# A layer of a graph network: one constant for the limits of the node buffer, four parts instead of five, lap operations at another place

## Chip, cores and metric

The kernel runs on one core of a Trainium2 chip. The metric is the device time of one execution in microseconds (us), lower is better.

## What is computed

The reference is one layer with three branches: a graph convolution over 106,250 edges between 6,250 nodes, a linear attention over the nodes, and a layer of two experts chosen by a router. Cut to what matters here, the graph branch is:

```python
m = src_feats[src_idx] @ weights[:d] + edge_feats @ weights[d:]
deg = jax.ops.segment_sum(jnp.ones((m.shape[0],)), dst_idx, num_segments=num_dst)
norm = jnp.where(deg > 0, jax.lax.rsqrt(jnp.maximum(deg, 1.0)), 0.0)
h = jax.ops.segment_sum(m * norm[dst_idx][:, None], dst_idx, num_segments=num_dst)
...
xn = _layernorm(x, axis=-1)
x = x + gnn(xn, edge_attr_256, src, dst, ...) + mix(xn[None], ...)[0]
x = x + ffn(_layernorm(x, axis=-1)[None], ...)[0]
```

`src_feats` is `xn` (6,250 x 256, float32), and the edges are sorted by their destination `dst`. Self loops are among them, so every node has at least one edge.

## The kernel before

**Edges and strips.** The sorted edges are cut into 277 strips (`NS`) of 384 edges (128 partitions x `TS` = 3), and four strips make a step, so there are 70 steps (`NG`), each of three loads of one edge per partition and strip. For a strip, POOL gathers the source rows from HBM by index (L554), SP loads the edge rows beside them (L418), and PE multiplies both by a one-hot matrix of 32 columns, one for each node from the strip's first (L887). This needs all destinations of a strip to lie within 32 nodes (`W`). The rows go through `ring`, which has six slots (`RS`). PE turns the strip's sums (L898), and DVE adds them into the node buffer `acc` at the row of the strip's first node (L1279); that row is read from `brow` into a register.

**The node buffer.** `acc` holds the sums of 5 x 250 nodes (`RC` x `CN` = `RN` = 1,250), and 32 more columns for strips that reach over its end. Node n stands at n modulo 1,250. The nodes are 25 parts of 250. When the last strip of a part has been added (`DONE`), DVE takes the degrees, ACT the root, DVE scales the part, PE projects it (`project`), ACT stores the result and clears the columns (`refill`). Before the strips of a step are added, DVE waits until the parts that are due have been cleared (`EMPTIED`, by the step alone). Where a part starts at column 0 again, `spill` (L1285, L1287) adds the 32 spare columns to the first 32 and clears them.

**The check.** The fast path is right only if each strip starts neither before the first part that is still open nor too far beyond it. `bwide` holds the first node of each strip. POOL writes two rows of 277 numbers, the lower limits `floor` (L547) and the upper limits `roof` (L550), by memsets of a few columns each; DVE subtracts, takes the maximum of both differences and reduces it to one flag, `ok_i`, which every engine reads at the end of the edge loop: with 0, a slow general path would run. `laps` counts how many times 1,250 goes into the first node, by one comparison for each lap (L1201, L1206); L1210 takes that off, and L1217 writes `brow`. `s_rel` is raised after `brow` and stands for all of it.

**The opening.** SP loads x in five blocks of ten tiles. DVE computes the statistics of each block (`stats`, L1133 to L1138), ACT takes the root, DVE the reciprocals (`scales`), and ACT normalises eight tiles and DVE two (`block_rest`, L1150). SP writes each block to the table `xn_table` in HBM. The order on DVE is written by hand: blocks 0, 1, 2, then the checks and laps, then blocks 3 and 4. Meanwhile POOL gathers the first 24 strips' rows from raw x into the ring. DVE takes their statistics in two halves (`raw_stats`), ACT the root of each half (L646), DVE the reciprocals (`raw_scales`, L1168), and ACT normalises twelve tiles of the ring for each half (L650). So DVE's second `raw_scales` waits until ACT has done the first half's twelve tiles. Then come `one_hot` (L1240) for step 0, the preparation of the weights, which SP loads behind the first six edge loads, the sum of two bias rows (L1267), and `one_hot` for step 1 in the loop.

Of the kernel before, what the change touches and what calls it, by code (L numbers as in the profile page):

```python
# [5 lines left out]
ALU = mybir.AluOpType  # L6
# [9 lines left out]
N = 6250  # L16
# [5 lines left out]
CN = 2 * TN  # L22
# [17 lines left out]
RC = 5  # L40
# [30 lines left out]
assert len(set(DONE)) == NC  # L71
# [9 lines left out]
def gps_layer(nc, x, src_l, dst_l, edges, wgnn, hbias, wkv_l, wq_t, bkv_l, bq_l, kln_g, kln_b, vln_g, vln_b,  # L81
              w1, b1_l, w2, b2, wr, br, fw1, fb1_l, fw2, fb2, gamma, beta, out):
    ctx = ExitStack()
    with ctx:
# [147 lines left out]
        roof = fl_t[:, :, :].rearrange("p c n -> p (c n)")[0:1, 0:NS]  # L232
# [10 lines left out]
        def wide(ap, n, m):  # L243
# [12 lines left out]
        s_id, s_const, s_iota, s_mask, s_d, s_dp, s_rel, s_wprep, s_roof, s_lap = (sem(f"s_{n}") for n in (  # L256
            "id", "const", "iota", "mask", "d", "dp", "rel", "wprep", "roof", "lap"))
# [270 lines left out]
        def _(pool):  # L528
# [19 lines left out]
            for e in sorted(set(EMPTIED)):  # L548
                lo, hi = EMPTIED.index(e) * ST, min((NG - EMPTIED[::-1].index(e)) * ST, NS)
                pool.memset(roof[0:1, lo:hi], float(CN * (e + RC) - W)).then_inc(s_roof, 1)  # L550

# [574 lines left out]
        def _(v):  # L1126
# [72 lines left out]
            v.wait_ge(s_roof, len(set(EMPTIED)))  # L1199
            v.tensor_tensor(roof[0:1, :], bwide[0:1, :], roof[0:1, :], ALU.subtract).then_inc(s_d, 1)  # L1200
            v.tensor_scalar(laps[0:1, 0, :], bwide[0:1, :], float(RN), None, ALU.is_ge).then_inc(s_lap, 1)  # L1201
            v.wait_ge(s_d, 11)
            v.tensor_tensor(floor[0:1, :], floor[0:1, :], roof[0:1, :], ALU.max).then_inc(s_d, 1)
            for k in range(2, N // RN + 1):
                v.wait_ge(s_lap, k - 1)
                v.scalar_tensor_tensor(laps[0:1, (k + 1) % 2, :], bwide[0:1, :], float(k * RN), laps[0:1, k % 2, :], ALU.is_ge, ALU.add).then_inc(s_lap, 1)  # L1206
            v.wait_ge(s_d, 12)
            v.tensor_reduce(okc[0:1, 5:6], floor[0:1, :], AX, ALU.max).then_inc(s_d, 1)
            v.wait_ge(s_lap, N // RN)
            v.scalar_tensor_tensor(laps[0:1, N // RN % 2, :], laps[0:1, (N // RN + 1) % 2, :], -float(RN), bwide[0:1, :], ALU.mult, ALU.add).then_inc(s_lap, 1)  # L1210
            v.wait_ge(s_d, 13)
            v.scalar_tensor_tensor(okc[0:1, 6:7], okc[0:1, 5:6], 0.0, okc[0:1, 4:5], ALU.is_le, ALU.mult).then_inc(s_d, 1)
# [427 lines left out]
```

## Time and profile before

| | us |
|---|---|
| median of three timed runs | 1610.42 |
| lowest and highest | 1605.93, 1611.3 |
| the profiled execution | 1606.38 |
| its span, first to last instruction | 1604.5 |

The page of the profile shows one execution. Its first part gives the busy time of each engine, its fourth the chain of work that ended last, followed back from the end. The windows give the busy time in chosen stretches, with the clock granted to PE as a share of full speed and the mean busy share of the DMA engines. An instruction's row has its start, its busy time, its line and operation, and in brackets how long its engine was idle before it and what ended that. "issue" and "remote" are idle times for which the profile names no instruction or transfer.

### The profile page before, as it was taken

The numbers are of one execution on the slowest core, as the hardware profiler recorded it, in microseconds if no ns is written. First come the engines' busy times: TensorE is split into PE (matmuls) and PEld (weight loads), VectorE is DVE, ScalarE is ACT, GpSimd is POOL, SyncE is SP. The second block draws the span as 40 slices with busy tenths as digits, with TensorE's granted clock in tenths as the row PEclk, the third lists the DMA queues.
The fourth block names the chain that finished last, engine by engine and source line by source line (L and its number), as shares of the span: only waits on it lengthen the run. The fifth ranks groups of instructions, "written<-read, shape, count | busy, mean of one in ns | idle before, by whom it ended". The sixth has DMA issues, their size and how long they took to land.

```text
span 1604.5 us, 19853 instructions
## 1 busy us (share of the span) xinstructions
PE 1070.4 (67%) x5959; PEld 659.1 (41%) x5959; DVE 757.2 (47%) x1750; ACT 539.1 (34%) x1100; POOL 933.1 (58%) x999
## 2 busy tenths in 40 slices
PE   0154775765677575666656675665666649999997
PEld 0011332322223222233333342333334349999997
DVE  5643453444544454423334343343343446677675
ACT  5511111211111111112233342343333356767673
POOL 6066766766776676666666667666676003434342
PEclk9977876868798787778867789787887869999999
DMA  9775655565665565487777778777776131111111
GB/s 270 261 227 164 199 182 180 173 191 174 193 185 182 172 195 171 142 248 208 219 217 229 216 246 249 210 232 227 222 249 202 46 93 28 50 46 44 50 39 40
DMA packets 189375, 275.65 MB, mean 172 GB/s; under 512 B 19840, under 2 KB 160296, under 8 KB 188037
## 3 DMA queue, kind: packets, MB, share of 16 engines
q1 hardware_dynamic: 139424, 152.85, 31.8%
q0 software_dynamic: 39888, 108.97, 22.6%
q10 hardware_dynamic: 9975, 12.80, 2.4%
q8 instruction: 37, 0.61, 0.2%
q14 instruction: 51, 0.42, 0.1%
HBM read 248.95 MB, written 25.60 MB: 171 GB/s over the span
## 4 chain that ended last, share of the span: by engine, by line
PE 37%; another core or an unknown queue 25%; issue 16%; DVE 12%; ACT 5%; DVEq 2%; DMA 1%; SPq 0%; ACTq 0%; POOL 0%; POOLq 0%
PE bank L1097 8%; PE bank L887 6%; PE bank L1086 5%; PE ps_t L1086 4%; PE bank L998 3%; PE bank L955 3%; PE bank L986 3%; PE bank L910 2%; DVEq L1277 2%; DVE acc L1279 2%; DVE lnst L1314 1%; DVE xc L1310 1%; PE ps_t L898 1%; PE bank L977 1%
## 5 line engine op out<-in xcount | busy, mean ns | idle before, releaser
L554 POOL DMA_INDIRECT ring<-xn_table,src_sb x807 | 798.2, 989 | 405.6 <-issue 225.4
L887 PE MATMUL bank<-ring,s 128*32 128x512 f32 x1662 | 285.8, 670 | 94.6 <-DVE s L1240 48.8
L955 PE MATMUL bank<-wstage,xt 128*125 128x512 f32 x200 | 135.6, 814 | 121.0 <-ACT xt L620 104.4
L1279 DVE TENSOR_TENSOR acc<-acc,ps_t 128x160 f32 x277 | 89.2, 322 | 141.2 <-issue 88.1
L887 PEld LDWEIGHTS bank<-ring,s 128*32 128x32 f32 x1662 | 42.8, 115 | 223.5 <-issue 166.5
L910 PE MATMUL bank<-wg,acc 128*125 128x256 f32 x400 | 102.2, 412 | 33.8 <-DVE acc L1302 29.8
L689 ACT ACTIVATE kvn<-xc 125x512 f32<-125x512 f32 x50 | 31.5, 630 | 263.6 <-DVE xc L1310 173.1
L1531 DVE TENSOR_TENSOR h_lo<-h,h_hi 128x512 fp32r<-128x512 f32 x100 | 95.7, 968 | 49.1 <-ACT h_hi L620 49.1
L1249 DVE TENSOR_TENSOR pair<-s 128x128 f32<-128x128 f32 x70 | 20.4, 292 | 208.5 <-remote 158.9
L609 POOL TENSOR_TENSOR rx<-vex,half 125x2 f32<-125x2 f32 x25 | 17.5, 701 | 171.9 <-DVE nmx L1552 171.9
L955 PEld LDWEIGHTS bank<-wstage,xt 128*125 128x125 f32 x200 | 44.1, 245 | 169.5 <-ACT xt L620 113.8
L1097 PE MATMUL bank<-fw_hi,h_hi 128*125 128x256 f32 x400 | 111.7, 279 | 0.0
L1097 PE MATMUL bank<-fw_hi,h_lo 128*125 128x256 f32 x400 | 111.7, 279 | 0.0
L1097 PE MATMUL bank<-fw_lo,h_hi 128*125 128x256 f32 x400 | 111.6, 279 | 0.0
L910 PEld LDWEIGHTS bank<-wg,acc 128*125 128x125 f32 x400 | 79.5, 204 | 73.3 <-DVE acc L1302 39.0
L998 PE MATMUL bank<-w_sb,hm 128*125 128x256 f32 x200 | 66.0, 487 | 59.7 <-ACT hm L704 37.9
L620 ACT ACTIVATE xt<-bank 128x250 f32<-128x250 f32 (+1 forms) x75 | 33.4, 445 | 198.1 <-remote 163.6
L1310 DVE TENSOR_TENSOR xc<-bank,bkv 125x512 f32<-125x512 f32 x50 | 34.4, 689 | 122.9 <-remote 108.5
L620 ACT ACTIVATE fl<-bank 128x512 f32<-128x512 f32 x70 | 41.2, 589 | 139.1 <-remote 102.0
L986 PE MATMUL bank<-xt,p_sb 128*128 128x250 f32 x200 | 61.8, 463 | 38.8 <-issue 37.2
L998 PEld LDWEIGHTS bank<-w_sb,hm 128*125 128x125 f32 x200 | 45.5, 239 | 92.2 <-ACT hm L704 45.9
L1097 PEld LDWEIGHTS bank<-fw_hi,h_hi 128*125 128x125 f32 x400 | 74.3, 186 | 0.0
(211 smaller groups left out, 2216.5 us busy)
## 6 DMA issues: line engine op xcount, KB each, us to landing
ring<-edges SPq DMA_DIRECT2D x207, 512.0 KB
ring<-xn_table,src_sb POOLq DMA_INDIRECT x807
xnr<-xn_table SPq DMA_DIRECT2D x25, 250.0 KB
xch<-x SPq DMA_DIRECT2D x25, 250.0 KB
base_rows<-xch ACTq DMA_DIRECT2D x25, 250.0 KB
xt_cols<-xte ACTq DMA_DIRECT2D x25, 250.0 KB
xtl<-xt_cols SPq DMA_DIRECT2D x25, 250.0 KB, 5.0
out<-res SPq DMA_DIRECT2D x25, 250.0 KB
```

The source lines that it names most:

```text
L554: pool.indirect_dma_start(out=to, out_offset=None, in_=rows, in_offset=bass.IndirectOffsetOnAxis(ap=index, axis=0),).then_inc(done, 16)
L620: return nc.scalar.activation(o, i, ACT.Copy)
L887: mm = pe.matmul(ps_seg[t % 2][j * W:(j + 1) * W, :], lhsT=s32[:, t % 3, j * TS + i, :], rhs=ring[:, u, j, :], start=i == 0, stop=i == TS ...
L910: mm = pe.matmul(ps_f[0:TN, j * D:(j + 1) * D], lhsT=acc[:, o, a:a + TN], rhs=wg[:, o, :], start=o == 0, stop=o == 2 * KC - 1)
L955: mm = pe.matmul(ps_kv[0:TN, :], lhsT=xt[:, n % 2, c, 0:TN], rhs=wstage[:, c, :], start=c == 0, stop=c == KC - 1)
L986: mm = pe.matmul(ps_kv[:, f * CW:f * CW + CN], lhsT=p_sb[:, o, f * P:(f + 1) * P], rhs=xt[:, (NT + c) % 2, o, :], start=o == 0, stop=o == ...
L998: mm = pe.matmul(ps_acc[0:TN, j * D:(j + 1) * D], lhsT=hm[:, f, j * TN:(j + 1) * TN], rhs=w2_sb[:, f, :], start=f == 0, stop=f == KC - 1)
L1086: mm = pe.matmul(bank[q][:, (f % 2) * CW:(f % 2 + 1) * CW], lhsT=a, rhs=b, start=n == 0, stop=n == len(ops) - 1)
L1097: mm = pe.matmul(ps_o[u][0:TN, j * D:(j + 1) * D], lhsT=a, rhs=b, start=n == 0, stop=n == len(ops) - 1)
L1279: v.tensor_tensor(acc[:, :, ds(b, W)], acc[:, :, ds(b, W)], planes[:, :, j * W:(j + 1) * W], ALU.add).then_inc(s_acc, 1)
L1310: v.tensor_tensor(xc[:, :], ps_kv[0:TN, :], bkv[:, :], ALU.add).then_inc(s_xc, 1)
L1531: v.tensor_tensor(h_lo[:, u, 2 * q:2 * q + 2, :], h32[:, 2 * q:2 * q + 2, :], h_hi[:, u, 2 * q:2 * q + 2, :].bitcast(F32), ALU.subtract).t ...
```

## The change

The buffer has four parts of 250 nodes instead of five (`RC`). The upper limits are gone, and POOL's 25 memsets with them: DVE subtracts the first nodes from `floor` and reduces the difference twice, to its maximum (which must not be above 0) and to its negated minimum (which must not be above 3 x 250 - 32 = 718). An assertion at build time says that the parts due to be cleared at a step are at most one behind the parts that are done. The flag now raises `s_rel`. The lap operations, one more of them because 1,000 goes into 6,250 six times, and the cast to `brow` stand between the two `raw_scales`, and raise a semaphore `s_ok` for which DVE waits before the first add.

```diff
-RC = 5
+RC = 4
...
-assert len(set(DONE)) == NC
+assert len(set(DONE)) == NC and all(EMPTIED[g] >= sum(d <= g for d in DONE[:-1]) - 1 for g in range(NG))
...
-            for e in sorted(set(EMPTIED)):
-                lo, hi = EMPTIED.index(e) * ST, min((NG - EMPTIED[::-1].index(e)) * ST, NS)
-                pool.memset(roof[0:1, lo:hi], float(CN * (e + RC) - W)).then_inc(s_roof, 1)
...
             v.tensor_tensor(floor[0:1, :], floor[0:1, :], bwide[0:1, :], ALU.subtract).then_inc(s_d, 1)
-            v.wait_ge(s_roof, len(set(EMPTIED)))
-            v.tensor_tensor(roof[0:1, :], bwide[0:1, :], roof[0:1, :], ALU.subtract).then_inc(s_d, 1)
-            v.tensor_scalar(laps[0:1, 0, :], bwide[0:1, :], float(RN), None, ALU.is_ge).then_inc(s_lap, 1)
-            v.wait_ge(s_d, 11)
-            v.tensor_tensor(floor[0:1, :], floor[0:1, :], roof[0:1, :], ALU.max).then_inc(s_d, 1)
-            for k in range(2, N // RN + 1):
-                v.wait_ge(s_lap, k - 1)
-                v.scalar_tensor_tensor(laps[0:1, (k + 1) % 2, :], bwide[0:1, :], float(k * RN), laps[0:1, k % 2, :], ALU.is_ge, ALU.add).then_inc(s_lap, 1)
+            v.wait_ge(s_d, 10)
+            v.tensor_reduce(okc[0:1, 5:6], floor[0:1, :], AX, ALU.max).then_inc(s_d, 1)
+            v.tensor_reduce(okc[0:1, 6:7], floor[0:1, :], AX, ALU.min, negate=True).then_inc(s_d, 1)
             v.wait_ge(s_d, 12)
-            v.tensor_reduce(okc[0:1, 5:6], floor[0:1, :], AX, ALU.max).then_inc(s_d, 1)
...
+            v.scalar_tensor_tensor(okc[0:1, 7:8], okc[0:1, 5:6], 0.0, okc[0:1, 4:5], ALU.is_le, ALU.mult).then_inc(s_d, 1)
             v.wait_ge(s_d, 13)
-            v.scalar_tensor_tensor(okc[0:1, 6:7], okc[0:1, 5:6], 0.0, okc[0:1, 4:5], ALU.is_le, ALU.mult).then_inc(s_d, 1)
+            v.scalar_tensor_tensor(okc[0:1, 5:6], okc[0:1, 6:7], float(CN * (RC - 1) - W), okc[0:1, 7:8], ALU.is_le, ALU.mult).then_inc(s_d, 1)
             v.wait_ge(s_d, 14)
-            v.tensor_copy(ok_i[:, :], okc[0:1, 6:7]).then_inc(s_d, 1)
...
-            v.tensor_copy(brow[0:1, :], laps[0:1, N // RN % 2, :]).then_inc(s_rel, 1)
+            v.tensor_copy(ok_i[:, :], okc[0:1, 5:6]).then_inc(s_rel, 1)
...
             raw_scales(0)
+            v.tensor_scalar(laps[0:1, 0, :], bwide[0:1, :], float(RN), None, ALU.is_ge).then_inc(s_lap, 1)
+            for k in range(2, N // RN + 1):
+                v.wait_ge(s_lap, k - 1)
+                v.scalar_tensor_tensor(laps[0:1, (k + 1) % 2, :], bwide[0:1, :], float(k * RN), laps[0:1, k % 2, :], ALU.is_ge, ALU.add).then_inc(s_lap, 1)
...
+            v.tensor_copy(brow[0:1, :], laps[0:1, N // RN % 2, :]).then_inc(s_ok, 1)
             raw_scales(1)
```

The order on DVE in the opening, from the subtraction of the first nodes to the statistics of block 3. Before (`fl` is `floor`, `fl_t` is `roof`, `kvn` holds `laps`):

```order
L1198 TENSOR_TENSOR fl<-fl,bwide 1x277
L1200 TENSOR_TENSOR fl_t<-bwide,fl_t 1x277
L1201 TENSOR_SCALAR kvn<-bwide 1x277
L1203 TENSOR_TENSOR fl<-fl,fl_t 1x277
L1206 SCALAR_TENSOR_TENSOR kvn<-bwide,kvn 1x277 x4
L1208 TENSOR_REDUCE okc<-fl 1x1
L1210 SCALAR_TENSOR_TENSOR kvn<-kvn,bwide 1x277
L1212 SCALAR_TENSOR_TENSOR okc<-okc 1x1
L1214 CAST ok_i<-okc 1x1
L1217 CAST brow<-kvn 1x277
L1219 CAST iota<-iota_i 128x128
L1133 BN_STATS st<-x 125x6 x10
```

Now:

```order
L1194 TENSOR_TENSOR fl<-fl,bwide 1x277
L1196 TENSOR_REDUCE okc<-fl 1x1
L1197 TENSOR_REDUCE okc<-fl 1x1
L1199 SCALAR_TENSOR_TENSOR okc<-okc 1x1
L1201 SCALAR_TENSOR_TENSOR okc<-okc 1x1
L1203 CAST ok_i<-okc 1x1
L1205 CAST iota<-iota_i 128x128
L1129 BN_STATS st<-x 125x6 x10
```

Nine operations left this place, and a second reduction and a second one-element combination came in.

Later on DVE, from the first `raw_scales` to the second and on to `one_hot` of step 0. Before:

```order
L1168 RECIPROCAL rg<-sdg 128x12
L1170 SCALAR_TENSOR_TENSOR nmrg<-mvg,rg 128x12
L1168 RECIPROCAL rg<-sdg 128x12
L1170 SCALAR_TENSOR_TENSOR nmrg<-mvg,rg 128x12
L1240 TENSOR_TENSOR s<-iota,rel 128x384
```

Now:

```order
L1164 RECIPROCAL rg<-sdg 128x12
L1166 SCALAR_TENSOR_TENSOR nmrg<-mvg,rg 128x12
L1216 TENSOR_SCALAR kvn<-bwide 1x277
L1219 SCALAR_TENSOR_TENSOR kvn<-bwide,kvn 1x277 x5
L1221 SCALAR_TENSOR_TENSOR kvn<-kvn,bwide 1x277
L1223 CAST brow<-kvn 1x277
L1164 RECIPROCAL rg<-sdg 128x12
L1166 SCALAR_TENSOR_TENSOR nmrg<-mvg,rg 128x12
L1234 TENSOR_TENSOR s<-iota,rel 128x384
```

The eight lap operations stand between the two.

In the edge loop the spills are at parts 4, 8, 12, 16, 20 and 24 instead of 5, 10, 15 and 20. On DVE at part 4, between the last add of a step and the degrees (`nrm`), the order now is:

```order
L1274 TENSOR_TENSOR acc<-acc,ps_t 128x5x32
L1280 TENSOR_TENSOR acc<-acc 128x5x32
L1282 MEMSET acc 128x5x32
L1289 TENSOR_SCALAR nrm<-acc 128x250
L1234 TENSOR_TENSOR s<-iota,rel 128x384
```

Two operations have come in there. On the other engines only POOL's 25 memsets of `fl_t` are gone, and ACT's first clearing of `acc` has 5,160 instead of 6,410 elements in a row. PE and SP have the same instructions in the same order.

## Rows read from the trace of the kernel before

**Rows 1.** The page, parts 1 and 4: busy time of the engines; the chain by engine

```profile
PE 1070.4 (67%) x5959; PEld 659.1 (41%) x5959; DVE 757.2 (47%) x1750; ACT 539.1 (34%) x1100; POOL 933.1 (58%) x999
...
PE 37%; another core or an unknown queue 25%; issue 16%; DVE 12%; ACT 5%; DVEq 2%; DMA 1%; SPq 0%; ACTq 0%; POOL 0%; POOLq 0%
```

**Rows 2.** Windows: length, busy time and instructions by engine, granted clock, DMA share, GB/s

```profile
60.00:80.00 20.00, 4.58 (x26) 1.12 (x26) 9.79 (x52) 12.77 (x28) 1.88 (x2) 1.00 0.98 309
400.00:1200.00 800.00, 523.33 (x2403) 258.18 (x2403) 329.50 (x772) 206.65 (x409) 546.28 (x554) 0.81 0.70 210
1300.00:1604.00 304.00, 286.26 (x2404) 285.48 (x2404) 200.69 (x360) 204.83 (x426) 106.60 (x100) 0.97 0.17 48
```

**Rows 3.** The chain of waits: start us, length us, what

```profile
67.99 6.00 ACT ring L650 x12
```

**Rows 4.** DVE's instructions: start, busy, operation, idle time before and its releaser

```profile
15.55 1.02 DVE L1179 TENSOR_TENSOR rel<-rel,bwide 128x831 f32<-128x831 f32 x1
...
35.01 0.43 DVE L1198 TENSOR_TENSOR fl<-fl,bwide 1x277 f32<-1x277 f32 x1
...
38.42 0.43 DVE L1203 TENSOR_TENSOR fl<-fl,fl_t 1x277 f32<-1x277 f32 x1 [2.41 <-remote]
39.83 0.43 DVE L1206 SCALAR_TENSOR_TENSOR kvn<-bwide,kvn 1x277 f32<-1x277 f32 x1 [0.97 <-remote]
42.62 0.44 DVE L1206 SCALAR_TENSOR_TENSOR kvn<-bwide,kvn 1x277 f32<-1x277 f32 x1 [2.36 <-issue]
44.02 0.43 DVE L1206 SCALAR_TENSOR_TENSOR kvn<-bwide,kvn 1x277 f32<-1x277 f32 x1 [0.96 <-issue]
44.71 0.44 DVE L1206 SCALAR_TENSOR_TENSOR kvn<-bwide,kvn 1x277 f32<-1x277 f32 x1 [0.26 <-issue]
45.08 0.42 DVE L1208 TENSOR_REDUCE okc<-fl 1x1 f32<-1x277 f32 x1
45.43 0.43 DVE L1210 SCALAR_TENSOR_TENSOR kvn<-kvn,bwide 1x277 f32<-1x277 f32 x1
...
46.67 3.33 DVE L1133 BATCH_NORM_STATS2 st<-x 125x6 f32<-125x256 f32 x10
```

**Rows 5.** Windows of the opening

```profile
40.00:45.00 5.00, 0.00 (x0) 0.00 (x0) 1.42 (x4) 0.00 (x0) 1.90 (x3) 1.00 0.93 363
45.00:50.00 5.00, 0.00 (x0) 0.00 (x0) 4.75 (x18) 0.00 (x0) 0.00 (x0) 1.00 0.20 75
50.00:55.00 5.00, 0.00 (x0) 0.00 (x0) 4.93 (x26) 3.82 (x9) 0.00 (x0) 1.00 0.55 178
55.00:60.00 5.00, 0.00 (x0) 0.00 (x0) 4.89 (x26) 4.12 (x10) 0.00 (x0) 1.00 0.74 240
```

**Rows 6.** Around the weights: waits, and instructions of DVE, PE and SP's queue

```profile
DVE st L1133 <- DMA x<-x: 4.7, 1, 4.7
...
50.79 0.73 DVE L1150 TENSOR_SCALAR x<-x,r,nmr 125x256 f32<-125x256 f32 x2
...
88.44 0.44 DVE L1267 TENSOR_TENSOR brows<-brows,hrows 125x256 f32<-125x256 f32 x1 [3.65 <-DMA hrows<-hbias]
...
89.58 1.94 PE L887 MATMUL bank<-ring,s 128*32 128x512 f32 x8 [9.93 <-issue]
...
62.03 8.01 SPq L418 DMA_DIRECT2D ring<-edges  x6
70.09 1.21 SPq L437 DMA_DIRECT2D wstage<-wkv_l  x1
```

**Rows 7.** DVE's wait for the second root

```profile
74.12 0.23 DVE L1168 RECIPROCAL rg<-sdg 128x12 f32<-128x12 f32 x1 [6.17 <-ACT sdg L646]
```

**Rows 8.** POOL's first gather

```profile
12.37 1.16 POOL L554 DMA_INDIRECT ring<-x,src_sb  x1 [6.26 <-issue]
```

**Rows 9.** DVE at the first spill, L1285 and L1287

```profile
401.21 0.33 DVE L1285 TENSOR_TENSOR acc<-acc 128x160 f32<-128x160 f32 x1
...
401.86 0.29 DVE L1294 TENSOR_SCALAR nrm<-acc 128x250 f32<-128x250 f32 x1
```

More of the change, by code:

```diff
@@ L231, in gps_layer @@
         floor = fl[0:1, 0:NS]
-        roof = fl_t[:, :, :].rearrange("p c n -> p (c n)")[0:1, 0:NS]
         laps = kvn[:, :, :].rearrange("p a d -> p (a d)")[0:1, 0:2 * NS].rearrange("p (a s) -> p a s", a=2)
@@ L255, in gps_layer @@
         s_gst, s_gmv, s_gve, s_gsd, s_grc, s_gr, s_raw = (sem(f"s_{n}") for n in ("gst", "gmv", "gve", "gsd", "grc", "gr", "raw"))
-        s_id, s_const, s_iota, s_mask, s_d, s_dp, s_rel, s_wprep, s_roof, s_lap = (sem(f"s_{n}") for n in (
-            "id", "const", "iota", "mask", "d", "dp", "rel", "wprep", "roof", "lap"))
+        s_id, s_const, s_iota, s_mask, s_d, s_dp, s_rel, s_wprep, s_ok, s_lap = (sem(f"s_{n}") for n in (
+            "id", "const", "iota", "mask", "d", "dp", "rel", "wprep", "ok", "lap"))
         s_e, s_gat = ([sem(f"s_{n}{u}") for u in range(RS)] for n in ("e", "gat"))
@@ L1229, in _ @@
             raw_scales(0)
+            v.tensor_scalar(laps[0:1, 0, :], bwide[0:1, :], float(RN), None, ALU.is_ge).then_inc(s_lap, 1)
+            for k in range(2, N // RN + 1):
+                v.wait_ge(s_lap, k - 1)
+                v.scalar_tensor_tensor(laps[0:1, (k + 1) % 2, :], bwide[0:1, :], float(k * RN), laps[0:1, k % 2, :], ALU.is_ge, ALU.add).then_inc(s_lap, 1)
+            v.wait_ge(s_lap, N // RN)
+            v.scalar_tensor_tensor(laps[0:1, N // RN % 2, :], laps[0:1, (N // RN + 1) % 2, :], -float(RN), bwide[0:1, :], ALU.mult, ALU.add).then_inc(s_lap, 1)
+            v.wait_ge(s_lap, N // RN + 1)
+            v.tensor_copy(brow[0:1, :], laps[0:1, N // RN % 2, :]).then_inc(s_ok, 1)
             raw_scales(1)
@@ L1269, in _ @@
             v.wait_ge(s_br, 1)
+            v.wait_ge(s_ok, 1)
             v.wait_ge(s_zero, 1)
```

4 lines of the change are left out of this document (removed).

## Prediction

> **What bounds the kernel now.** I read the page first, then the chain of waits in order of time, then the instructions of each engine in order of time around the changed lines. The page says that no engine is full over the whole span: PE is busy for 67% and POOL for 58% [rows 1]. The windows show three stages: an opening with hardly any matmul work up to 75 us, the edge loop up to about 1250 us with the DMA engines 70% busy over most of it, and an expert stage in which PE runs 286 of 304 us [rows 2]. The change touches the first, and two instructions more in the second; the third stays as it is.
>
> In the opening the chain of waits lies on DVE from the first block of x on: statistics, the checks, statistics again, then ACT's first twelve scalings of the ring at 67.99 us [rows 3]. In that chain the checks and lap operations, lines 1198 to 1219, take the stretch from 35.01 us to the next statistics at 46.67 us, 11.66 us [rows 4]. Little of it is work: five waits in brackets before these operations, 2.41, 0.97, 2.36, 0.96 and 0.26 us, make 6.96 us. Each of these operations waits for a semaphore that DVE's own previous operation raises; elsewhere such a wait is invisible (45.08 to 45.43 us). All the stalls that I see there end before 44.7 us, while the DMA engines are still 0.93 busy; from 45 us they are 0.20 busy and the stalls are gone [rows 4, 5].
>
> **What the checks lose.** Out of the stretch go the subtraction for the upper limit (L1200), the first comparison (L1201), the maximum (L1203), four lap comparisons (L1206), the lap product (L1210) and the cast to the row numbers (L1217). A second reduction and a second one-element operation come in. Without a stall, a 277-element operation costs 0.35 us from start to start (45.08 to 45.43) [rows 4]; I let the one-element ones cost no more. The new stretch is the subtraction, two reductions, two combinations and the flag's cast, 6 x 0.35 = 2.1 us, and the cast of iota, which stays as it is. That is 11.66 - 2.1 = 9.6 us less if no stall is left, and 9.6 - 7.0 = 2.6 us less if all of them return on other operations. These are the bounds of the main term.
>
> Between them: ten operations of the old stretch wait for DVE's own results and lose 6.96 us, 0.7 each; five of them lose 1.4 each. The new stretch has four such waits (first reduction, both combinations, the flag's cast), which makes 2.8 to 5.6 us of stall, and a gain of 4.0 to 6.8 us. Another way is to lay the new operations over the old stalls where they stood in time: the reductions run until 36.15 us, the first combination waits until 38.42, the second until 39.83, and the statistics begin at 40.4 us, 6.3 us early. I take 6.0 us.
>
> **Whether 6 us of DVE arrive at the end of the opening.** Block 3 of x must have landed at 40.4 us instead of 46.67; DVE waits for a block of x only once, before the first [rows 6], which says that block 3 is there by 46.67, not since when. The write of block 2 of the table follows DVE's last tiles of that block at 51.5 us [rows 6] and would come at 45.5 us. Between 45 and 60 us the DMA engines have 5 x (0.80 + 0.45 + 0.26) = 7.6 us free [rows 5], so that 6 us fit, but 9.6 would not quite: the gathers that now end by 47 us would share the engines with it. Behind it SP issues the edge loads from 62.03 and the weights from 70.09 us; the last row that DVE needs lands at 88.44 us, and behind it stands one_hot(1), for which PE's fourth group of strips waits until 89.58 us [rows 6]. From 60 to 80 us the DMA engines are 0.98 busy [rows 2], thus this part shifts with its start and doesn't shrink. A cap of about 7 us follows for any DVE gain, 6.0 passes.
>
> **The moved lap operations** stand between the two halves of the ring's scales, where DVE waits from 67.95 to 74.12 us, 6.17 us, for ACT's root [rows 7]. The first comparison, five instead of four further ones (1,000 goes into 6,250 six times), the product and the cast are 8 x 0.35 = 2.8 us. They cost nothing as long as they stay under 6.17 us. If stalls like those of the opening came back here, 2.8 + 7.0 = 9.8 us would pass the cover by 3.6 us, which would then delay ACT's second twelve tiles and one_hot(0). For it: the DMA engines are 0.98 busy there too [rows 2]. Against it: no operation of DVE that follows in the next twenty microseconds is late by its own predecessor; the ones that wait name a DMA or ACT [rows 6, 7].
>
> **POOL and ACT** lose the 25 memsets of L550 and a fifth of the clearing of acc. POOL's first gather starts 6.26 us after its last memset [rows 8], so the gathers may start sooner by the memsets' time or not at all; DVE reads what they bring only after all five blocks, ACT has nothing to do before DVE's first variance. I count zero for both.
>
> **The smaller buffer.** It spills at every fourth part of 250 nodes, thus six times instead of four. One spill pushes DVE's next operation from 401.21 to 401.86 us: 0.65 us [rows 9]. Two more are 1.3 us at most, and zero where DVE is waiting anyway. I take 0.6. The waits of the adds for emptied parts are by EMPTIED, which is the same table as before, so the smaller buffer brings no new wait.
>
> **The addresses.** All tiles behind acc move down by 5,024 bytes (20,640 instead of 25,640 bytes for acc, rounded up), so the ring starts 224 instead of 128 bytes above a multiple of 256. No row here shows a transfer to another start. The Trainium skill, DMA: Bandwidth & Descriptors, section How a descriptor splits into AXI transactions, speaks against this: a descriptor that starts off a 256-byte boundary is fetched from the boundary below, so that, if it held for writes into the ring as well, a row of 1,024 bytes would cost 39 beats of 32 bytes and not 36. I take zero and keep the case as a rival.
>
> **Sum.** -6.0 + 0.6 = -5.4 us. The profiled execution took 1606.38 us (span 1604.5), so 1601.0 for such a one. The three timed runs lie at 1605.93 to 1611.3 around a median of 1610.42; the profiled one is 4.0 below that, which by the median would give 1605.0. Between the two I say 1603.5.
>
> **Rivals.**
> 1. *The stalls return* on whatever waits in that window: gain 2.6 - 0.6 = 2.0 us, about 1607. For it: they lie in one stretch of time, the last before the DMA engines empty [rows 4, 5]. Against: there are fewer waits left to suffer.
> 2. *The stalls belonged to the removed operations*: they stand before operations with a scalar or a second operand from SBUF, none before the reduction or the statistics [rows 4]. Then up to 9.6 us go, of which the DMA engines pass about 7 to 9: 1600. The Trainium skill, SBUF — State Buffer, section Who interferes with whom, has such a rule: a DVE operation with two SBUF inputs or in a two-port mode is locked out while GpSimd holds the pair, a reduction never. The trace agrees only in part, since POOL generates gathers from 12.37 us on [rows 8], and the subtraction at 15.55 us, with two operands from SBUF, shows no stall [rows 4].
> 3. *The edge loop swallows it*: the loop waits on landings and on PE's granted clock (0.81 there, between its two levels of 1.2 and 2.4 GHz) [rows 2], so 6 us sooner in need not be 6 us sooner out: 1608 to 1610.
> 4. *Slower, by the addresses*: 25% of the chain is waits for an unknown queue, which in the loop are the gathers' and edges' landings [rows 1]. Transfers 5% longer would make 0.05 x 0.25 x 1604 = 20 us, 1622; from 1.4% on (5.4 us) it eats the gain.
> 5. *The new check refuses the data* and the general path runs: milliseconds. By the reference's own draw the first node of a strip is at most 394 above its lower limit, where 718 are allowed, and never below it; the flag stays 1.
>
> **Chances.** Forecast, 4 to 7 us carried through: 0.45. Rival 2: 0.15. Rival 1: 0.13. Rival 3: 0.17. Rival 4: 0.09, of which half under 1611. Rival 5 and others: 0.01. All run to run within some 2.5 us. A measurement of this kernel tells about 0.3%, 4.8 us, from no change: faster means under 1605.6. That holds for rival 2, two thirds of the forecast and a little of the others: 0.5. Slower, over 1615.3: 0.08. Same: 0.42. The range that leaves out two in ten goes from rival 2 with its scatter to rival 3: 1598 to 1611.
>
> **What would show it.** Right: statistics of block 3 start near 40.4 us (36.9 at the least, 44 at the most); ACT's ring tiles near 62 and 68.6 us with the lap operations inside DVE's wait; one_hot(1) near 82.5 us; PE's expert stage begins 5 us sooner and lasts as long. Wrong: the stalls on the new reductions, lap operations past the root, one_hot(1) at 88 us in spite of an earlier start (the DMA cap), or an edge loop that is longer by what the opening saves; for rival 4, a loop longer by 10 us or more with gathers' waits grown all over it.

## The result, and the profile after

| | before | after |
|---|---|---|
| median of 19 timed runs, us | 1607.81 | 1603.32 |
| lowest and highest | 1602.61, 1613.23 | 1597.46, 1610.02 |
| the profiled execution | 1606.38 | 1610.02 |
| its span | 1604.5 | 1608.2 |

The ratio after to before is 0.9972, with a 95% interval of 0.996 to 0.9983: 4.5 us less. The nineteen executions of after spread over 12.6 us, and the profiled one is the longest of them, so its length says nothing about the change; what can be read from it is where things stand in it. The page's parts 1 and 4, the answer to [rows 1]:

```profile
PE 1053.9 (66%) x5959; PEld 653.6 (41%) x5959; DVE 757.3 (47%) x1755; ACT 537.5 (33%) x1100; POOL 929.4 (58%) x974
...
another core or an unknown queue 31%; PE 30%; issue 14%; DVE 11%; ACT 8%; DMA 2%; DVEq 2%; SPq 2%; ACTq 0%; POOL 0%; POOLq 0%
```

The windows of after, for [rows 2] and [rows 5] (length, busy time and instructions of PE, PEld, DVE, ACT, POOL, granted clock, DMA share, GB/s):

```profile
60.00:80.00 20.00, 5.66 (x26) 1.20 (x26) 8.61 (x34) 12.99 (x27) 5.64 (x6) 0.97 1.01 302
400.00:1200.00 800.00, 504.63 (x2401) 250.79 (x2399) 324.67 (x764) 204.52 (x405) 548.11 (x554) 0.80 0.70 211
...
40.00:45.00 5.00, 0.00 (x0) 0.00 (x0) 4.90 (x23) 2.73 (x6) 0.00 (x0) 1.00 1.01 266
45.00:50.00 5.00, 0.00 (x0) 0.00 (x0) 4.93 (x25) 4.20 (x9) 0.00 (x0) 1.00 1.02 418
```

In the middle of the loop, instructions, clock (0.80 against 0.81) and DMA share are as before; PE shows 19 us less busy time there, which I leave unexplained. In the opening, DVE is busy for 4.90 of the 5 us from 40 us on, where before it had 1.42, and the quiet of the DMA engines behind 45 us (0.20) is gone.

DVE's instructions around the checks, for [rows 4] (start, busy, operation, in brackets the idle time before it and its releaser):

```profile
29.08 3.36 DVE L1129 BATCH_NORM_STATS2 st<-x 125x6 f32<-125x256 f32 x10
...
33.63 0.31 DVE L1132 BATCH_NORM_AGGREGATE mvs<-st 125x2 f32<-125x6 f32 x3 [1.04 <-DVE st L1129]
...
35.76 0.18 DVE L1132 BATCH_NORM_AGGREGATE mvs<-st 125x2 f32<-125x6 f32 x1 [1.21 <-remote]
...
38.00 0.17 DVE L1134 TENSOR_SCALAR ve<-mvs 125x10 f32<-125x10 f32 x1 [1.23 <-DVE mvs L1132]
...
39.44 0.43 DVE L1194 TENSOR_TENSOR fl<-fl,bwide 1x277 f32<-1x277 f32 x1
39.90 0.43 DVE L1196 TENSOR_REDUCE okc<-fl 1x1 f32<-1x277 f32 x1
40.26 0.42 DVE L1197 TENSOR_REDUCE okc<-fl 1x1 f32<-1x277 f32 x1
...
41.28 3.35 DVE L1129 BATCH_NORM_STATS2 st<-x 125x6 f32<-125x256 f32 x10
```

The stretch from the subtraction to the next statistics takes 41.28 - 39.44 = 1.84 us, where it took 11.66, and no wait is left in it. But it begins 4.4 us later than before (39.44 against 35.01). The stalls now stand before it, on the aggregation of block 2, an operation that has no scalar, yet they are not the reason: before the change 4.6 us of stall stood between the statistics of block 2 and the stretch as well (the 1.75, 1.81 and 1.06 us below), and now there are 4.4. The reason is that the statistics of block 2 begin 4.15 us later, at 29.08 us instead of 24.93. Before:

```profile
24.93 3.36 DVE L1133 BATCH_NORM_STATS2 st<-x 125x6 f32<-125x256 f32 x10
...
30.71 0.17 DVE L1138 TENSOR_SCALAR ve<-mvs 125x10 f32<-125x10 f32 x1 [1.75 <-remote]
...
33.52 0.17 DVE L1144 SCALAR_TENSOR_TENSOR nmr<-mvs,r 125x10 f32<-125x10 f32 x1 [1.81 <-remote]
...
34.94 0.14 DVE L1197 TENSOR_SCALAR okc<-okc 1x1 f32<-1x1 f32 x1 [1.06 <-issue]
```

Out of 9.8 us less in the stretch come 5.4 us at its end (41.28 against 46.67). Over the whole opening up to 50 us, DVE's stalls of 0.2 us or more, without its waits for loads, add up to 11.8 us before and 4.4 us after.

DVE in its wait for the second root, for [rows 7], and the step to `one_hot` of step 1, for [rows 6]:

```profile
62.89 0.29 DVE L1216 TENSOR_SCALAR kvn<-bwide 1x277 f32<-1x277 f32 x1
63.22 2.32 DVE L1219 SCALAR_TENSOR_TENSOR kvn<-bwide,kvn 1x277 f32<-1x277 f32 x5
65.57 0.44 DVE L1221 SCALAR_TENSOR_TENSOR kvn<-kvn,bwide 1x277 f32<-1x277 f32 x1
66.04 0.30 DVE L1223 CAST brow<-kvn 1x277 int32<-1x277 f32 x1
69.15 0.23 DVE L1164 RECIPROCAL rg<-sdg 128x12 f32<-128x12 f32 x1 [2.82 <-ACT sdg L642]
69.50 0.55 DVE L1234 TENSOR_TENSOR s<-iota,rel 128x384 f32<-128x384 f32 x1
...
88.23 0.42 DVE L1261 TENSOR_TENSOR brows<-brows,hrows 125x256 f32<-125x256 f32 x1 [5.31 <-issue]
88.75 0.56 DVE L1234 TENSOR_TENSOR s<-iota,rel 128x384 f32<-128x384 f32 x1
```

The eight lap operations take 62.89 to 66.34 us and leave 2.82 us of the wait: they are hidden. The sum of the bias rows comes no earlier than before (88.23 against 88.44). The chain of waits of after no longer passes ACT's ring tiles as in [rows 3]; it goes over SP's queue to the last row that this sum needs (start, length, what), although `one_hot` of step 0 is 5 us earlier (69.50 against 74.47):

```profile
58.05 2.16 SPq L417
...
77.16 0.62 SPq L445
...
77.83 7.85 DMA hrows<-hbias
```

POOL's last memset and its first gather, for [rows 8]; DVE at the first spill, for [rows 9]:

```profile
3.67 1.05 POOL L546 MEMSET fl<- 1x16 f32 x25
4.91 1.16 POOL L550 DMA_INDIRECT ring<-x,src_sb  x1 [0.18 <-issue]
```

```profile
343.48 0.33 DVE L1280 TENSOR_TENSOR acc<-acc 128x160 f32<-128x160 f32 x1
...
344.13 0.29 DVE L1289 TENSOR_SCALAR nrm<-acc 128x250 f32<-128x250 f32 x1
```

The first gather starts 7.5 us earlier than before, by far more than the 1.43 us that the removed memsets were busy. I had not expected that, and most of the study turns on it.

### The profile page after: what moved, and what is told of

It reads as the page before. It is cut to its first block, busy times and chain, and to the rows that moved or that the text cites. A ratio compares the mean times of both kernels' runs of the same rounds, so it can differ in the third digit from the quotient of the medians.

```text
span 1608.2 us, 19835 instructions
## 1 busy us (share of the span) xinstructions
PE 1053.9 (66%) x5959; PEld 653.6 (41%) x5959; DVE 757.3 (47%) x1755; ACT 537.5 (33%) x1100; POOL 929.4 (58%) x974
## 4 chain that ended last, share of the span: by engine, by line
another core or an unknown queue 31%; PE 30%; issue 14%; DVE 11%; ACT 8%; DMA 2%; DVEq 2%; SPq 2%; ACTq 0%; POOL 0%; POOLq 0%
PE bank L1093 8%; PE bank L1082 5%; PE ps_t L1082 4%; PE bank L883 3%; PE bank L951 3%; PE bank L906 2%; DVEq L1272 2%; PE bank L982 1%; DVE acc L1274 1%; DVE lnst L1309 1%; DVE nrm L1295 1%; DVE xc L1305 1%; PE bank L994 1%; DMA x<-x 1%
## 5 line engine op out<-in xcount | busy, mean ns | idle before, releaser
L550 POOL DMA_INDIRECT ring<-xn_table,src_sb x807 | 795.7, 986 | 416.4 <-issue 223.4
L883 PE MATMUL bank<-ring,s 128*32 128x512 f32 x1662 | 279.1, 678 | 82.8 <-DVE s L1234 53.3
L605 POOL TENSOR_TENSOR rx<-vex,half 125x2 f32<-125x2 f32 x25 | 17.5, 701 | 171.9 <-DVE nmx L1547 171.9
L616 ACT ACTIVATE xt<-bank 128x250 f32<-128x250 f32 (+1 forms) x75 | 33.5, 446 | 236.7 <-remote 198.3
L994 PE MATMUL bank<-w_sb,hm 128*125 128x256 f32 x200 | 62.0, 460 | 55.5 <-ACT hm L700 31.6
L594 POOL TENSOR_TENSOR xlb<-xl,b2w 125x512 f32<-125x512 f32 x25 | 32.4, 1297 | 73.2 <-DVE b2w L1589 73.2
```

The source lines that it names most:

```text
L550: pool.indirect_dma_start(out=to, out_offset=None, in_=rows, in_offset=bass.IndirectOffsetOnAxis(ap=index, axis=0),).then_inc(done, 16)
L616: return nc.scalar.activation(o, i, ACT.Copy)
L883: mm = pe.matmul(ps_seg[t % 2][j * W:(j + 1) * W, :], lhsT=s32[:, t % 3, j * TS + i, :], rhs=ring[:, u, j, :], start=i == 0, stop=i == TS ...
L994: mm = pe.matmul(ps_acc[0:TN, j * D:(j + 1) * D], lhsT=hm[:, f, j * TN:(j + 1) * TN], rhs=w2_sb[:, f, :], start=f == 0, stop=f == KC - 1)
```

## The experiments

I call "gate" the first gather from the table (L550 with `xn_table`), with which the edge loop's stream of gathers starts: 77.81 us before, 72.84 after. PE's first group of strips releases it:

```profile
72.84 0.95 POOL L550 DMA_INDIRECT ring<-xn_table,src_sb  x1 [37.60 <-PE bank L883]
```

In the table below, all times are us from the start of the span of one profiled execution each; the ratios are against the kernel before on the same chip, that of after from the result above and those of e1 to e10 from five timed rounds. e11 and e12 are profiles only. "Raw gathers" are the start of the first and the last of the 24 gathers from raw x; "last stall" is the last operation of DVE before 50 us that begins 0.2 us or more late after DVE's own previous one; "hot 1" is the start of `one_hot` for step 1; "25th" the 25th gather from the table.

| kernel | raw gathers | last stall | statistics of block 4 | gate | hot 1 | 25th | ratio, 95% interval |
|---|---|---|---|---|---|---|---|
| before | 12.37, 41.56 | 46.14 | 51.77 | 77.81 | 88.97 | 112.50 | 1 |
| before, again (e11) | 12.65, 42.29 | 44.24 | 49.70 | 75.75 | 86.62 | 108.90 | |
| after | 4.91, 34.29 | 38.00 | 46.39 | 72.84 | 88.75 | 108.33 | 0.9972, 0.996 to 0.9983 |
| e1 buffer of five parts | 4.91, 34.66 | 38.64 | 47.70 | 73.74 | 85.87 | 107.25 | 0.9978, 0.9965 to 0.999 |
| e3 old addresses | 4.91, 34.86 | 38.19 | 46.80 | 72.84 | 84.68 | 106.34 | 0.9977, 0.9964 to 0.999 |
| e6 bias rows later | 4.92, 34.16 | 38.55 | 47.21 | 73.25 | 81.13 | 107.35 | 0.998, 0.9965 to 0.9994 |
| e8 and weights sooner | 4.92, 34.44 | 38.49 | 46.86 | 72.91 | 76.77 | 106.50 | 0.9977, 0.9963 to 0.9991 |
| e2 memsets back | 12.08, 41.61 | 46.04 | 47.51 | 73.56 | 86.48 | 107.16 | 0.9998, 0.9982 to 1.0013 |
| the same again (e12) | 13.11, 42.20 | 45.34 | 50.65 | 76.69 | 89.51 | 110.10 | |
| e5 gathers held | 11.73, 41.60 | 46.04 | 47.09 | 73.13 | 86.48 | 107.23 | 1.0, 0.9984 to 1.0016 |
| e4 laps in front | 4.91, 34.51 | 38.95 | 50.69 | 76.73 | 89.05 | 110.24 | 1.0002, 0.9987 to 1.0016 |
| e7 memsets and laps in front | 13.21, 42.18 | 46.88 | 55.16 | 81.20 | 93.27 | 115.21 | 1.0012, 0.9998 to 1.0026 |
| e9 `one_hot(0)` sooner | 4.91, 34.79 | 38.63 | 47.01 | 69.80 | 87.33 | 106.88 | 0.9988, 0.9973 to 1.0002 |
| e10 that and e8 | 4.92, 34.51 | 38.59 | 46.00 | 68.78 | 76.07 | 102.41 | 0.9958, 0.9942 to 0.9974 |

All edits are against the changed kernel. The kernel before measured 1619.49 us on the chip of e1 to e4, 1606.85 beside e5 to e8 and 1605.29 beside e9 to e12.

**e1: the buffer of five parts again.**

```diff
-RC = 4
+RC = 5
```

> The changed kernel with five parts in the buffer (1,250 nodes) instead of four: new check, moved lap operations, four spills. Theory A (the gain is made in the opening, the smaller buffer costs two spills of 0.65 us): 3.5 to 5.5 us below before, up to 1.3 us better than the changed kernel, ratio about 0.997. Rival (the smaller buffer and the moved addresses have a price of their own): 8 us or more below before. DVE's first statistics of block 3 start within 1 us of 41.3 us.

Measured 1615.25 us. Beside the changed kernel's 0.9972, or beside e3 (four parts, 1616.19 us on the same chip), there is no difference that can be told: the gain is not in the buffer, and its two more spills cost at most some 2 or 3 us. A spill takes 0.65 us in the trace of after (343.48 to 344.13). The statistics of block 3 start at 42.59 us, a little outside the 1 us that I had allowed.

**e2: POOL's memsets again**, with nobody reading them (the lines that declare their row and semaphore are left out here).

```diff
+            for e in sorted(set(EMPTIED)):
+                lo, hi = EMPTIED.index(e) * ST, min((NG - EMPTIED[::-1].index(e)) * ST, NS)
+                pool.memset(roof[0:1, lo:hi], float(CN * (e + RC) - W)).then_inc(s_roof, 1)
```

> The changed kernel with POOL's 25 memsets of the upper limits put back (nothing reads them). Theory A (POOL's 25 instructions moved its first gather from 12.37 to 4.91 us, so that the gathers take bandwidth from the blocks of x): the first gather is at 12 to 13 us again, the first block of x is there at 10.7 us instead of 13.2, statistics of block 3 start at 36.5 to 38 us, and the time is 0 to 3 us below the changed kernel's. Rival (the start of the first gather is chance): it starts at 6 to 7 us, right behind the memsets, and nothing else moves.

Measured 1618.71 us. The whole gain is gone (0.9998), and my expectation with it: I had said 0 to 3 us below the changed kernel. The early marks came out (first block of x at 10.84 us, statistics of block 3 at 36.49), so an early block 3 is not an early end. POOL's first gather is back at 12 us:

```profile
4.68 1.43 POOL L550 MEMSET fl_t<- 1x20 f32 x25
12.08 1.16 POOL L554 DMA_INDIRECT ring<-x,src_sb  x1 [5.97 <-issue]
```

And the stalls are back, on what the new check is made of and on the statistics of block 3:

```profile
32.07 0.43 DVE L1200 TENSOR_REDUCE okc<-fl 1x1 f32<-1x277 f32 x1 [0.79 <-DVE fl L1198]
...
34.18 0.15 DVE L1203 SCALAR_TENSOR_TENSOR okc<-okc 1x1 f32<-1x1 f32 x1 [1.33 <-DVE okc L1201]
35.57 0.15 DVE L1205 SCALAR_TENSOR_TENSOR okc<-okc 1x1 f32<-1x1 f32 x1 [1.25 <-DVE okc L1203]
...
41.14 0.43 DVE L1133 BATCH_NORM_STATS2 st<-x 125x6 f32<-125x256 f32 x1 [0.96 <-issue]
...
43.24 0.18 DVE L1136 BATCH_NORM_AGGREGATE mvs<-st 125x2 f32<-125x6 f32 x1 [1.22 <-remote]
```

**e3: the ring at its old addresses.**

```diff
+        pad = sbs("pad", [P, 1256])
```

> The changed kernel with 5,024 unused bytes behind acc, so that every tile behind it has the address that it had before the change. If the addresses count: 5 us or more away from the changed kernel (0.997 of before) on either side. If not: 0.996 to 0.998 of before, with the same start times in the opening within 1 us.

Measured 1616.19 us, 0.9977: no difference from the changed kernel. The statistics of block 3 start at 41.69 us, 0.4 from those of after. Rival 4 falls. The Trainium skill, DMA: Bandwidth & Descriptors, section How a descriptor splits into AXI transactions, would give 39 beats instead of 36 for such a start; for writes into the ring no run here shows a price.

**e4: the eight lap operations ahead of the cast of iota** again, though behind the check and not woven into it as before the change; the rest stays. The first of the eight lines:

```diff
+            v.tensor_scalar(laps[0:1, 0, :], bwide[0:1, :], float(RN), None, ALU.is_ge).then_inc(s_lap, 1)
...
             raw_scales(0)
-            v.tensor_scalar(laps[0:1, 0, :], bwide[0:1, :], float(RN), None, ALU.is_ge).then_inc(s_lap, 1)
```

> The changed kernel with the eight lap operations back in front of the statistics of block 3. Theory A (their 2.8 to 3.1 us lie on the path there, but the loads behind are bound by the DMA engines): ring scalings and one_hot of step 0 start 3 us later than in the changed kernel, one_hot of step 1 and the time only 0 to 1.5 us later. Rival (DVE's path is what counts): both 3 us later and the time 3 us above the changed kernel, ratio about 0.999.

Measured 1618.66 us, 1.0002: this gives the gain back as well, as the rival in the expectation has it. No lap operation is stalled here; they stand behind the stalls and cost their work, 42.09 to 45.45 us:

```profile
42.09 0.28 DVE L1204 TENSOR_SCALAR kvn<-bwide 1x277 f32<-1x277 f32 x1
42.41 2.32 DVE L1207 SCALAR_TENSOR_TENSOR kvn<-bwide,kvn 1x277 f32<-1x277 f32 x5
...
45.45 0.21 DVE L1213 CAST iota<-iota_i 128x128 f32<-128x128 int32 x1
45.59 0.73 DVE L1129 BATCH_NORM_STATS2 st<-x 125x6 f32<-125x256 f32 x2
```

**e5: no memsets, but POOL waits before its first gather** until block 0 of x is there.

```diff
+            pool.wait_ge(s_x[0], 32)
```

> The changed kernel, but POOL waits for the first block of x (two of its semaphore's transfers) before the first gather; its instructions are otherwise those of the changed kernel. Theory A (late gathers are what made the kernel with the 25 memsets lose its gain): first gather at 10.7 to 12.5 us, ratio 0.999 to 1.000, as with the memsets. Theory B (not the time of the gathers, but something else about the memsets, or scatter): ratio 0.997 to 0.998 as in the changed kernel.

Measured 1606.3 us, 1.0. So it isn't the memsets' being there that costs but the late gathers: held to 11.73 us by a wait, they undo the gain in the same way. The stretch of the check takes only 2.65 us here (30.84 to 33.49); the stalls stand behind it, on the statistics and aggregations of block 3, the last at 46.04 us. The profile is of the shortest of e5's twelve executions (1603.3 us, their median is 1606.3), so it shows a better opening than the timing does.

**e6: the sum of the bias rows from ahead of the edge loop to DVE's step 6.**

```diff
-            v.wait_ge(s_par, 16 * 11)
-            v.tensor_tensor(brows[:, :], brows[:, :], hrows[:, :], ALU.add).then_inc(s_br, 1)
...
+                if q == 6:
+                    v.wait_ge(s_par, 16 * 11)
+                    v.tensor_tensor(brows[:, :], brows[:, :], hrows[:, :], ALU.add).then_inc(s_br, 1)
+                    v.wait_ge(s_br, 1)
```

> The changed kernel with the sum of the two bias rows, and its wait for the last of the weights, moved behind the second step of the edge loop. If the loads capped what the opening passes on (one_hot of step 1 waits for the last row): one_hot of step 1 at 82 to 84 us instead of 84.7 to 89 and the time 2 to 4 us below the changed kernel, ratio 0.995 to 0.996. If the edge loop's own pace is what counts: ratio 0.997 to 0.998, as in the changed kernel.

Measured 1603.41 us, 0.998. `one_hot` of step 1 comes 7.6 us earlier (81.13), and nothing is won over the changed kernel that can be told; I had said 0.995 to 0.996 if the loads were the cap.

**e7: e2 and e4 together**, so both parts undone, while the one-constant check and the smaller buffer stay.

> The changed kernel with both put back: POOL's 25 memsets and the lap operations in front. What is left of the change is the one-constant check (less by two operations of 0.35 us and their waits) and the smaller buffer (two spills more, 1.3 us). If the parts add up: the memsets' and the laps' 3 to 4 us each would make it 2 to 4 us slower than before, ratio 1.0015 to 1.0025. If they replace each other: 1.000 within 0.001.

Measured 1608.75 us, 1.0012. The new check and the smaller buffer alone bring nothing; if anything they lie above the kernel before (the interval, 0.9998 to 1.0026, just holds 1).

**e8: e6, and SP loads the weights `wkv` and `bkv` behind the third edge load.**

```diff
-            for q in range(RAW):
+            for q in range(TS):
...
+            for q in range(TS, RAW):
+                edge_load(q)
```

> As the one with the bias rows moved, and SP loads the key and value weights behind the third edge load instead of the sixth. DVE's preparation of the weights starts at 70 to 72 us instead of 79 to 81, one_hot of step 1 at 75 to 78 us. If the start of the loop passes through: 2 to 5 us below the one with the bias rows moved, ratio 0.992 to 0.994. If the ring's fourth slot and the gathers bound it then: 0 to 2 us.

Measured 1603.05 us, 0.9977. `one_hot` of step 1 is at 76.77, 12 us earlier than in the changed kernel, and again nothing comes of it, as in the second case of the expectation.

**e9: `one_hot(0)` with its strip counts ahead of the second `raw_scales`**, thus under the rest of the wait for the root.

```diff
-            raw_scales(1)
...
+            raw_scales(1)
```

> The changed kernel with one_hot(0) and its strip counts ahead of the second raw_scales. Both stand then inside DVE's wait for the root (62.89 to 69.15 us in the changed kernel), so one_hot(0) should run near 66.5 instead of 69.50 us and PE's first strips near 67 instead of 70.11. Theory, what counts is when POOL's table gathers start: if they are released by PE's first strips, they start 3 us earlier, near 70 instead of 72.84 us, and the kernel takes 3 us less than the changed one: a ratio to the kernel before of 0.995. Rival, PE's first strips need ACT's second twelve tiles of the ring anyway, which now come after a later second raw_scales: table gathers near 72.8 or later, ratio 0.997 to 0.998. Other rival, the start of the table gathers is not what counts: gathers earlier and the ratio still 0.997 to 0.998.

Measured 1603.12 us, 0.9988. The gate opened at 69.80 us, 3 us earlier, as the theory says, but the ratio did not follow: my number, 0.995, lies outside the interval. The 25th gather stands at 106.88, no earlier than in e3 with its gate at 72.84. What is late now is `one_hot` of step 1 at 87.33 us, behind the bias rows, for which PE waits:

```profile
67.07 5.26 PE L883 MATMUL bank<-ring,s 128*32 128x512 f32 x24 [37.72 <-DVE s L1233]
...
87.95 1.94 PE L883 MATMUL bank<-ring,s 128*32 128x512 f32 x8 [15.25 <-DVE s L1233]
```

**e10: e9 and e8 together.**

> The edit of e9 together with those of e8 (bias rows later on DVE, weights wkv behind the third edge load). By the theory that the start of the table gathers counts, the same as e9: ratio 0.995, since e8 alone brought nothing over the changed kernel (0.9977). If one_hot(1) were the limit once one_hot(0) is earlier, e10 is 2 us or more below e9.

Measured 1600.05 us, 0.9958: 3.1 us below e9, as the last sentence of the expectation has it. PE now waits 6.13 us, not 15.25, and the 25th gather is at 102.41 us, the earliest of all:

```profile
66.06 4.14 PE L885 MATMUL bank<-ring,s 128*32 128x512 f32 x24 [38.24 <-DVE s L1235]
...
76.69 1.94 PE L885 MATMUL bank<-ring,s 128*32 128x512 f32 x8 [6.13 <-DVE s L1235]
```

It has the lowest ratio of the study. Its interval overlaps that of the changed kernel, with which it was not timed on one chip, so that it beats that one is likely and not shown; it beats the kernel before.

**e11: the kernel before once more**, one profile.

> The kernel before, unchanged, for a second look at its opening. If one profile of an opening is typical: first gather 12 to 13 us, the stretch of the checks 10 to 12 us with five or so stalls of about 7 us in all, statistics of block 3 near 46.7, first table gather near 77.8 us. If it is not: the table gathers start anywhere from 73 to 78 us, and differences of 3 us between single profiles mean nothing.

The stretch takes 12.17 us (32.42 to 44.59), against 11.66, but starts 2.6 us earlier, and the gate is at 75.75 us. One profile of an opening of this kind is good to some 2 or 3 us.

**e12: the kernel of e2 once more**, one profile.

> The kernel of e2 again (the change with POOL's 25 memsets put back), for the same reason: its first profile had the first gather at 12.08 and the first table gather at 73.56 us, as early as the changed kernel's 72.84, while it was timed no faster than the kernel before (0.9998). If one profile is typical, table gathers again near 73.5; if the first profile was a lucky one, up to 77 us.

The gate is at 76.69 us, 3.1 us later than in the first profile of e2, and the one profile is no more typical than the other. The stalls stand on the new operations, on a reduction too:

```profile
38.34 0.14 DVE L1197 TENSOR_SCALAR okc<-okc 1x1 f32<-1x1 f32 x1 [2.42 <-remote]
...
40.45 0.43 DVE L1200 TENSOR_REDUCE okc<-fl 1x1 f32<-1x277 f32 x1 [1.53 <-remote]
...
42.54 0.15 DVE L1203 SCALAR_TENSOR_TENSOR okc<-okc 1x1 f32<-1x1 f32 x1 [1.31 <-DVE okc L1201]
43.94 0.15 DVE L1205 SCALAR_TENSOR_TENSOR okc<-okc 1x1 f32<-1x1 f32 x1 [1.25 <-issue]
45.34 0.14 DVE L1207 CAST ok_i<-okc 1x1 int32<-1x1 f32 x1 [1.25 <-DVE okc L1205]
```

**What they say together.** In the table, the last stall lies between 38.00 and 38.95 us in all eight profiles in which the raw gathers start at 4.9 us, and between 44.24 and 46.88 us in all six in which they start at 11.7 to 13.2, whatever instructions stand there. The stalls are a stretch of time that ends 2 to 5 us after POOL's last raw gather, and e5, which moves nothing but the gathers, moves that end. They don't end with the transfers: in after the packets of POOL's queue still take 40, 28, 22 and 8.5% of the DMA engines' time in the four windows of 5 us from 40 to 60 us, and the engines are full (1.01 and 1.02) from 40 to 50 us, without a stall of DVE. A full set of DMA engines alone, as in rival 1, is thus not what stalls it. From the statistics of block 4 to the gate there are 26.04 or 26.05 us in eleven of the twelve kernels and profiles with `one_hot(0)` in its place (26.45 in after), and 22.8 in e9 and e10. So the gate is set by the end of the stalled stretch and by the work of DVE that remains behind it.

By the timed medians on one chip: late gathers cost 2.5 to 3.5 us (e2 against e3 and e1) or 2.9 to 3.3 us (e5 against e6 and e8); laps in front cost 2.5 to 3.4 us (e4 against e3 and e1) and, with late gathers, 2.4 us (e7 against e5), which twelve executions on each side hardly tell from nothing. Against the kernel before, either part alone gives nothing (e4, and e2 and e5), and both give the 4.5 us; since the kernel without either, e7, stands 1.9 us above the kernel before, that adds up within the errors.

Behind the gate, the 25th gather comes 33.5 us after it or 19.6 us after `one_hot` of step 1, whichever is later. I took both numbers from the table (e3: 72.84 to 106.34; after: 88.75 to 108.33). Together they give the other twelve within 0.7 us, except the first profile of before (1.2 us late): e9 by the second (106.93, measured 106.88), e10 by the first (102.28, measured 102.41). They are a fit and not a mechanism, and the second is tested by e9 alone. From the 25th to the 701st gather it then takes 975.8 to 977.6 us in ten profiles and 986.3 to 986.8 in the four of e1 to e4, wherever the loop started. The last 106 gathers take anything from 155.3 to 163.8 us, with no order by kernel that I can see, and that hides the gain in the profile of after: there they take 160.7 us, in the first profile of before 156.2. Of these 4.5 us, 4.4 lie in the last 16 gathers (30.7 against 26.3 us), in waits of POOL of which the last three are, in after:

```profile
1237.54 0.94 POOL L550 DMA_INDIRECT ring<-xn_table,src_sb  x1 [2.49 <-remote]
1242.98 0.94 POOL L550 DMA_INDIRECT ring<-xn_table,src_sb  x1 [4.50 <-PE bank L883]
1246.39 0.94 POOL L550 DMA_INDIRECT ring<-xn_table,src_sb  x1 [2.47 <-PE bank L883]
```

Behind the last gather another 2.4 us are lost in that profile: PE's expert stage begins at 1308.80 us instead of 1305.38, and lasts 299 us in both. The last add of the loop waits there for ACT's clearing of the buffer, 7.02 us after the change against 4.08 before:

```profile
1269.80 0.32 DVE L1274 TENSOR_TENSOR acc<-acc,ps_t 128x160 f32 x1 [7.02 <-ACT acc L616]
```

That is not the price of four parts: with four parts this wait is 4.12 or 4.13 us in six profiles (e2, e4, e7, e9, e10, e12) and 5.8 to 7.0 us in five.

## Why the prediction was right, and where it was not

**The number**: 1603.5 forecast, 1603.32 measured. A good part of that is luck: the main term came out only as the sum of two errors that cancel, and of the marks by which I wanted to know it, two failed (`one_hot` of step 1 at 88.75 us, where 88 was my sign of being wrong, and in the profile an expert stage that begins 3.4 us later instead of 5 us sooner).

**The stretch without stalls** was put at 2.1 us and took 1.84 with the cast of iota. The price of 0.35 us was right for the operations on 277 elements (0.36 to 0.46 from start to start); the one-element ones took 0.18.

**The stalls** were the weak step. I laid the new operations over the old stalls "where they stood in time" and took them for fixed in time; they belong to the gathers' time, and this moved by 7.5 us. The stretch lost 9.8 us and not 6.0, a little more than my upper bound of 9.6, and block 3 came only 5.4 us earlier because block 2 came 4.15 us later, a term that I had put at zero. Nor do the stalls end before 44.7 us, as I read them: one of 0.22 us stands at 46.14, where the DMA engines are already 0.20 busy. With the gathers late as before, the stretch took 5.64 us in e2 (30.85 to 36.49) and 7.13 in e12, inside 4.9 to 7.7 (2.1 and 2.8 to 5.6 of stall), but 2.65 us in e5, where it lay ahead of most stalls. And yet e2 and e5 were timed no faster than before. A gain inside the stretch of 4.0 to 6.8 us was therefore no gain at the end: rival 1, in a harder form, for the next operations, statistics and aggregations of block 3, then have the stalls. In the single profiles of e2 and e5 a part came out all the same (see what stays open).

**POOL** "may start sooner by the memsets' time or not at all; ... I count zero" failed. The memsets of L550 held the first gather back by 7.5 us, and e2 and e5 show that without its earlier start the change brings nothing. My reason, that DVE reads what the gathers bring only after all five blocks, is true and beside the point: the gathers act on DVE by the stalls while they run, not by their data. There is a price too, which I had not counted: the second block of x comes later under early gathers. From DVE's first statistics to those of block 1 it takes 6.7 to 7.6 us in the eight profiles with early gathers (7.59 in after, with a wait of 1.71 us for the load) and 5.8 to 6.1 in the six others. The rest of the 4.15 us at block 2 is the first block, at 13.18 us instead of 10.69; that is scatter, since it starts at 10.6 to 11.5 us in the other seven early profiles.

**The laps** were put at 2.8 us, under the root's wait. They take 3.4 us, all hidden; e4 shows what they cost in the open, 3.4 us on DVE and 2.5 to 3.4 on the whole. In my sum the laps had no term of their own: they were in the 6.0. This part of the mechanism was right.

**The cap by the weights**, "about 7 us", was a real mechanism with the wrong shape. I took it for something that moves with SP's start. In after it did not move: the bias rows came at 88.23 in spite of edge loads that SP began 4 us earlier, and by the two numbers above it cost 108.33 - 106.34 = 2 us at the 25th gather. In e1 and e3 the rows came earlier and it cost nothing; e6 and e8, which take it away, win nothing that the timing can tell. By the two numbers it binds when `one_hot` of step 1 comes more than 13.9 us after the gate: 15.9 us in after, 17.5 in e9, whose timed median is 3.1 us above that of e10, where it is 7.3.

**Rival 2**, stalls that belong to operations with a second operand, falls: in e12 and e2 they stand before reductions, in after and e2 before aggregations and statistics. The Trainium skill, SBUF — State Buffer, section Who interferes with whom, exempts a reduction from the lock; the 1.53 us before a reduction that reads one row in e12 are not explained by it. **Rival 3**, the loop swallows it: not in the timed medians, and not between the 25th and the 701st gather, but in a single profile its end can, and did. **Rival 4** fell with e3, **rival 5** didn't occur.

**The smaller buffer** was put at 0.6 us. Two more spills at 0.65 us are 1.3, one of them in the open behind the last adds (at 1270.15 us in after, where there was none); e1 can't tell it from nothing.

**What stays open.** Late gathers with the laps moved gave gates of 73.56, 73.13 and 76.69 us in three profiles, two of them as early as the changed kernel's, and yet e2 and e5 were timed 2.5 to 3.5 us slower than their early counterparts. The two early ones are profiles of executions 1.4 and 3.0 us below the median of their kernel, which may be all there is to it; with single profiles I can't say whether 76.69 is the usual one. The early kernels lie within 72.84 to 73.74 in five of five. So that late gathers cost 3 us is shown by the timings, and the way through the gate is argued. What in the gathers stalls DVE is open too; by the traces it ends with POOL's issuing of them and not with their transfers. And I don't know why 25 small memsets delay what follows them by 6 us. The traces hold a hint: in all five profiles with these memsets a packet of the instruction queue (q14, about 8 KB) starts at 9.7 to 10.9 us, 2.3 to 2.5 us ahead of the first gather, and no other stands between 3 and 14 us; in the eight with early gathers none comes before 17.4 us. A wait for instructions would look like this, but no run here moves that packet by itself.

## What to carry to other kernels

When waits of an engine for its own results come in a cluster, look for what else runs in just that time and how it ends, before pricing the instructions on which they fall: taking instructions out of the cluster can just let others fall in (e2, e5), while ending its cause sooner, or moving work into a wait that has another reason (the laps under ACT's root), shortens it. Ask of every removed instruction on a side engine what stood behind it in its queue, even if it was cheap. And where single profiles scatter by as much as the gain, find the stretch that doesn't (here from block 4 to the gate, and from the 25th gather to the 701st) and place the gain before or behind it.

## What the runs showed of the hardware

- 25 memsets that fill 277 numbers of one row, 1.43 us busy, delay POOL's first gather from 4.91 or 4.92 us (eight profiles) to 12.08 to 13.21 us (five profiles). The profile names no releaser for the 6 us behind them ("issue"); in each of the five a packet of the instruction queue starts 2.3 to 2.5 us ahead of the gather.
- While POOL issues gathers and x is loaded, from 22 us on at the earliest (e9) though the gathers start at 4.91 us, DVE's operations begin late behind its own previous one: by up to 1.36 us where the profile names DVE's previous result (e5), 3.03 us where it names nothing (e7) and 4.74 us where it names a remote releaser (e8, before the variance of block 2); before reductions, statistics and aggregations as before operations with scalars. This ends 2 to 5 us after the last of these gathers is issued (14 profiles), and in after some 20 us before their last transfers.
- The same kernel differs by 0.8% from chip to chip: 1619.49 against 1606.85 us for the kernel before. Of these 12.6 us, some 9.5 lie between the 25th and the 701st gather (about 986.5 against 977 us, from the profiles of the changed kernels e1 to e4 and of the others).
